# Feature blocks inside the sort rounds, half the count sums from PSUM, and two head rows loaded earlier

## What is computed

```python
x = layernorm(x + gat(x))          # 8 heads of 64: softmax over in-edges, batch norm, gelu, skip product
x = layernorm(x + tensor_prod(x))  # per-edge MLP (8 -> 64 -> 64 -> 64 -> 512), products with x[src], sum by dst
x = layernorm(x + kan_gat(x))      # one-head attention, then silu and 8 spline bases, each times 512 x 512
x = layernorm(x + sage(x))         # mean of neighbours, product 512 x 1024, relu
```

## Time and profile before

| what | before |
| --- | --- |
| median of 3 runs | 1746.64 us (1743.93 to 1747.52) |
| profiled execution: time | 1744.53 us |
| profiled execution: span | 1742.6 us |
| busy: TensorE, VectorE, ScalarE, GpSimd | 1470.6, 1321.9, 727.0, 499.8 us |
| mean granted clock of TensorE | 0.932 of full |

### The profile page before, as it was taken

How to read it: one execution, slowest core, us unless ns; L and a number is a source line. 1 busy time by engine, 2 the same in 40 slices (tenths; PEclk the granted TensorE clock), 3 DMA queues, 4 the chain that set the end, 5 groups by cost and what they waited for, 6 DMA issues and landing times.

```text
span 1742.6 us, 24098 instructions
## 1 busy us (share of the span) xinstructions
PE 1470.6 (84%) x7759; PEld 794.3 (46%) x7759; DVE 1321.9 (76%) x2036; ACT 727.0 (42%) x1595; POOL 499.8 (29%) x490
## 2 busy tenths in 40 slices
PE   2888998174878783799999999869899989999997
PEld 1465545022433332655655555745444434444443
DVE  8796999968999998499998999788377357724232
ACT  1285664075555553455554555431244134312000
POOL 1788888700010001255665664000000000002000
PEclk9889998587999996899999999979999999999999
DMA  4101000143120201455665666001011121210000
GB/s 150 31 6 9 6 6 6 35 144 87 55 73 30 72 15 39 136 169 172 189 182 166 180 190 123 1 0 49 0 58 62 48 73 48 72 72 0 12 18 29
DMA packets 67195, 122.74 MB, mean 70 GB/s; under 512 B 12613, under 2 KB 31159, under 8 KB 67010
## 3 DMA queue, kind: packets, MB, share of 16 engines
q0 software_dynamic: 22944, 58.12, 13.3%
q1 hardware_dynamic: 42748, 59.87, 10.6%
q10 hardware_dynamic: 1446, 4.03, 0.7%
HBM read 106.57 MB, written 15.22 MB: 70 GB/s over the span
## 4 chain that ended last, share of the span: by engine, by line
PE 48%; DVE 19%; POOL 14%; issue 11%; ACT 4%; DMA 3%; DVEq 1%; SPq 0%; ACTq 0%; another core or an unknown queue 0%; POOLq 0%
PE PS L1175 18%; POOL recs L641 14%; PE PS L1060 7%; DVE arena L1811 6%; PE PS L1223 5%; PE PS L1143 5%; PE PS L1046 4%; DVE arena L1807 3%; ACT arena L1486 2%; PE PS L1219 2%; PE PS L1211 2%; DVE arena L1775 2%; DVE arena L1947 1%; PE PS L1111 1%; DVE cnt_d L1581 1%
## 5 line engine op out<-in xcount | busy, mean ns | idle before, releaser
L1175 PE MATMUL PS<-arena 128*125 128x512 f32 x720 | 314.4, 600 | 12.1 <-ACT arena L1545 6.6
L641 POOL DMA_INDIRECT recs<-arena x170 | 249.0, 1464 | 90.6 <-issue 90.0
L1486 ACT ACTIVATE arena<-arena,gslot 128x32 f32<-128x32 f32 x832 | 185.3, 308 | 170.9 <-DVE arena L1930 81.6
L1060 PE MATMUL PS<-arena 128*32 128x128 f32 (+1 forms) x3328 | 231.3, 308 | 18.4 <-issue 7.9
L688 POOL DMA_INDIRECT arena<-xup,gidx x208 | 197.6, 950 | 141.8 <-DVE arena L1939 62.0
L1060 PEld LDWEIGHTS PS<-arena 128*32 128x32 f32 x3328 | 174.5, 110 | 127.5 <-issue 73.3
L977 PE MATMUL PS<-arena 125*128 125x512 f32 (+1 forms) x480 | 190.6, 535 | 44.0 <-DVE arena L1811 44.0
L1175 PEld LDWEIGHTS PS<-arena 128*125 128x125 f32 x720 | 136.8, 190 | 189.2 <-issue 189.2
L1939 DVE TENSOR_TENSOR arena<-PS,arena 128x768 f32<-128x768 f32 x208 | 196.7, 946 | 0.0
L695 POOL CAST arena<-cnt_s 125x1250 f32<-125x1250 uint16 x10 | 12.6, 1303 | 495.3 <-PE PS L1175 495.3
L977 PEld LDWEIGHTS PS<-arena 125*128 125x128 f32 x480 | 86.1, 192 | 148.5 <-issue 78.2
(11 more groups left out here) (311 smaller groups left out, 2008.2 us busy)
## 6 DMA issues: line engine op xcount, KB each, us to landing
arena<-in_spline_wT SPq DMA_DIRECT2D x16, 1024.0 KB, 5.3
arena<-uv_rows SPq DMA_DIRECT2D x14, 610.4 KB
arena<-h_rows SPq DMA_DIRECT2D x26, 256.0 KB
h_rows<-arena SPq DMA_DIRECT2D x24, 256.0 KB, 2.8
arena<-xup,gidx POOLq DMA_INDIRECT x208
recs<-arena POOLq DMA_INDIRECT x170
xup<-arena SPq DMA_DIRECT2D x10, 250.0 KB
out<-x_sb SPq DMA_DIRECT2D x10, 250.0 KB
```

What stands on the lines that cost most here:

```text
L641: pool.indirect_dma_start(out=recs, out_offset=bass.IndirectOffsetOnAxis(pos[:, c:c + 1], 0), in_=rec[:, c, :], in_offset=None).then_inc(s ...
L1060: ins = t.matmul(PS[quad * DB:(quad + 1) * DB, bank, o0 * MUL:o0 * MUL + w], sel4[:, s, v * DB:(v + 1) * DB], prod[:, s, c0 * MUL:c1 * MUL ...
L1175: ins = t.matmul(PS[:NP, b, :], basis[:, slot, (k * HB + b) * NP:(k * HB + b + 1) * NP], w_sp[:, slot, k * D:(k + 1) * D], start=(first an ...
L1486: ins = A(sel4[:, s, y * DB:(y + 1) * DB], eq4[:, m // 4, s * DB:(s + 1) * DB], ACT.Copy, scale=gslot[:, par, c + R_Y + y:c + R_Y + y + 1])
```

## The change

The sort's feature blocks 6 to 9 move into the rounds, after rounds 1, 4, 7 and 10 (`GIN`), with their copies one round later on ScalarE. In the last TAIL = 4 rounds VectorE writes `lane_dl` itself, with a float16 copy of `dl1`. Of the count sums, the even pairs still go through ScalarE and `cnt_ev` (two buffers now); the odd ones VectorE adds to `cnt_d` straight from PSUM. The rows of heads 6 and 7 are loaded after pieces 1 and 5 of the MLP, not 9 and 15. The first loads of `gld` and `h3` stand ahead of the `xup` writes in SyncE's queue. GpSimd zeroes `acc` when the last product of the attention is done, not after the first gelu half.

```diff
@@
 SBUFS = 3
+TAIL = 4
+GIN = (1, 4, 7, 10)
 NSPL = 8
@@
         PR = SB // 2
-        dl1 = at(6200, [NP, EC])
+        dl1, dl1_h = at(6200, [NP, EC]), at(6374, [NP, EC], f16)
         iota2 = sb("iota2", [128, 2 * NT], f16)
@@
         rec_sb = at(9300, [128, NDG, 2 * GT * RW])
-        cnt_ev = at(28300, [NP, 3, HALF], u16)
+        cnt_ev = at(28300, [NP, 2, HALF], u16)
+
+        def bucket_sums(n):
+            return PS[:NP, 2 * (n % 3):2 * (n % 3) + 2, :].rearrange("p a n -> p (a n)")[:, 0:HALF]
@@
                 hidden_out(n)
-                if n in (9, 15):
-                    load_row(HROWS + 2 + (n - 9) // 6)
+                if n in (1, 5):
+                    load_row(HROWS + 2 + n // 5)
             sp.wait_ge(s_uvrow_ok, 1)
@@
             sp.dma_start(a2r[:], a["L2_gnn_a"].rearrange("(r p) k -> r (p k)", p=128)).then_inc(s_wl2_in, 16)
-            for b in range(NB):
-                sp.wait_ge(s_xup_cp, b + 1)
-                sp.dma_start(xup[b * NP:(b + 1) * NP, :], xup_st[:, b % 2, :]).then_inc(s_xup_out0 if b % 2 == 0 else s_xup_out1, 16)
-
             def load_h3(pair, par):
@@
                 load_h3(par, par)
+            for b in range(NB):
+                sp.wait_ge(s_xup_cp, b + 1)
+                sp.dma_start(xup[b * NP:(b + 1) * NP, :], xup_st[:, b % 2, :]).then_inc(s_xup_out0 if b % 2 == 0 else s_xup_out1, 16)
             with sp.Fori(0, G // 4 - 1) as i:
@@
-            pool.wait_ge(s_gelu_ok, 1)
+            pool.wait_ge(s_pv_done, WR + H * NB)
             pool.memset(acc, 0.0).then_inc(s_acc_zero, 1)
@@
                 pe.wait_ge(s_sort_ok, j + 1)
-                pe.wait_ge(s_lane_cp, j + 1)
+                pe.wait_ge(s_lane_cp, min(j + 1, ROUNDS - TAIL))
                 for n in range(SB):
@@
             gat_block(HB)
-            for b in range(HB + 1, NB - 2):
-                gat_block(b)
             pe.wait_ge(s_order_cp, 2)
                 sort_batch(j)
-                if j in (3, 8):
-                    gat_block(NB - 2 + j // 8)
+                if j in GIN:
+                    gat_block(NB - len(GIN) + GIN.index(j))
                 if j == ROUNDS - 4:
@@
                     pe.wait_ge(s_oha_ok, n // WP + 1)
-                if n >= 3:
-                    pe.wait_ge(s_cnt_left, n - 2)
+                if n >= 3 and (n - 3) % 2 == 0:
+                    pe.wait_ge(s_cnt_left, (n - 3) // 2 + 1)
+                elif n >= 3:
+                    pe.wait_ge(s_cnt_flushed, n - 2)
                 for e in range(2):
@@
                 ins.then_inc(s_cntt_ps, 1)
-            pe.wait_ge(s_cnt_left, NPAIR)
+            pe.wait_ge(s_cnt_flushed, NPAIR)
             max_rows(0)
@@
-            for b in range(HB, NB - 2):
-                gat_out(b)
+            gat_out(HB)
@@
             for j in range(ROUNDS):
-                scale_lanes(j)
-                if j in (4, 9):
-                    gat_out(NB - 2 + j // 9)
+                if j < ROUNDS - TAIL:
+                    scale_lanes(j)
+                if j - 1 in GIN:
+                    gat_out(NB - len(GIN) + GIN.index(j - 1))
                 if j == ROUNDS - 3:
@@
                 act.wait_ge(s_cnt_ps, n + 1)
-                if n >= 3:
-                    act.wait_ge(s_cnt_flushed, n - 2)
-                psv = PS[:NP, 2 * (n % 3):2 * (n % 3) + 2, :].rearrange("p a n -> p (a n)")[:, 0:HALF]
-                A(cnt_ev[:, n % 3, :], psv, ACT.Copy).then_inc(s_cnt_left, 1)
+                if n >= 4:
+                    act.wait_ge(s_cnt_flushed, n - 3)
+                A(cnt_ev[:, n // 2 % 2, :], bucket_sums(n), ACT.Copy).then_inc(s_cnt_left, 1)
             for n in range(NPAIR):
-                counts_out(n)
+                if n % 2 == 0:
+                    counts_out(n)
                 if n == 1:
@@
             v.tensor_copy(tile_f, tile_i)
+            v.tensor_copy(dl1_h, dl1)
             link(v.tensor_copy(lane_f, lane_i))
@@
                 dve.wait_ge(s_lane_ok, j + 1)
+                if j >= ROUNDS - TAIL:
+                    v.tensor_tensor(lane_dl[:, rs], lane_oh[:, rs], of_pairs(dl1_h, 128), ALU.mult)
                 v.tensor_tensor(lane_src[:, rs], lane_oh[:, rs], of_pairs(src_f, 128), ALU.mult).then_inc(s_sort_ok, 1)
@@
             def flush_counts(n, word):
-                dve.wait_ge(s_cnt_left, n + 1)
+                if n % 2 == 0:
+                    dve.wait_ge(s_cnt_left, n // 2 + 1)
+                else:
+                    dve.wait_ge(s_cnt_ps, n + 1)
                 if n >= 1:
                 dstv = cnt_d[:, bass.ds(k * HALF, HALF)]
-                v.tensor_tensor(dstv, cnt_ev[:, n % 3, :], dstv, ALU.add).then_inc(s_cnt_flushed, 1)
+                v.tensor_tensor(dstv, cnt_ev[:, n // 2 % 2, :] if n % 2 == 0 else bucket_sums(n), dstv, ALU.add)\
+                    .then_inc(s_cnt_flushed, 1)
             for n in range(NPAIR + 2):
                     dst_onehots(n // WP)
```

## The result

The kernel after takes 1749.38 us in the median of 19 runs, the kernel before 1744.48 in the 19 runs beside it. The ratio is 1.0027, with a 95% interval of 1.0014 to 1.0040: 4.7 us slower (2.4 to 7.0). The forecast was 1742.5 us and, for likeliest, faster. In changes, 4.1 us less was forecast and 4.7 more came. The time lies inside the range of 1731 to 1752, the sign is wrong. The profiled execution took 1746.28 us (span 1744.4), 1.8 more than that of before.

The account below looks back on a forecast made before the run. Before the attention, VectorE's line (rounds, counts, maxima) raced scatter, load and MLP, VectorE 12 us behind. Terms: attention +0.5, zeroing -3.4, queue -1.2, sum -4.1 us; 1746.64 - 4.1 = 1742.5, range 1731 to 1752.

Parts of the forecast that it names:

- Counts: Count stage on VectorE: 52 odd sums read from PSUM take 799 instead of 476 ns, 16.8 us more.
- The bound of 22: Upper bound in us on the extra cost of the counts, if each PSUM sum also waits 0.1 for TensorE.
- The prediction's own sign of being wrong: Count stage: a PSUM sum well under 800 ns, or a subtraction that waits for the memset, would show the forecast wrong.
- Sort: Sort rounds: TensorE ends at 140.4 instead of 142.5, taken as -2.3 us on VectorE's line, bounds 0 and -6.8.
- Rows of heads 6 and 7: Maxima and MLP: 14.24 us of standing go, but MLP writes queue behind row 7; attention +0.5 us.
- Zeroing: Before layer 1's first scaling: the memset, moved to 662.6, leaves the chain, -3.4 us, no cost beside subtractions and inversion.
- a memset that blocks the subtractions or the inversion: Rival at the moved memset: subtractions wait, sum +7.1 us (1753.7), or only the inversion, +5.0 (1751.6); chance 0.15.
- Queue before the messages: Start of the message loop: with `gld` loaded long before, copies and first gather come earlier, -1.2 us, bounds 0 and -1.4.
- Cheap PSUM sums: Rival in the counts: extra below 2 us, sum -16.9, time 1729.7; with half the extra, 1734; chance 0.19.
- The stand in SyncE's queue costs more: Rival before the attention: PSUM sums cost 22 us or write backlog delays ScalarE; sum -1 to +1.5, 1745.6 to 1748; chance 0.16.
- The base: Starting time for the whole kernel: the profiled execution, 1744.53 us, with the median of the runs 2.1 above, 1746.64.

## Why the prediction failed, point by point

**Counts: the term that was mis-sized, and the cause of the wrong sign.** The sum had 16.8 us, priced from the earlier trace rows as 0.323 x 52. That price was right: (794 - 476) ns x 52 = 16.5 us. The step that failed is the next one: it took this for the whole growth of the stage and held everything else in it constant, with no term for the instructions beside the sums. There was the error: the one-hots beside it went from 389 to 425 ns, 0.036 x 208 = 7.5 us, and 16.5 + 7.5 = 24.0 is what the stage grew in the profiled pair, with other differences below 1 us.

One pair is not the typical one. The kernel before took 127.9 us for the stage in its own profile and 129.0 to 130.2 in the six others with all sums by ScalarE and the full scatter, and the five profiled runs with sums from PSUM beside the full scatter took 150.1 to 151.9, so the typical growth is nearer 21. It is made of the 16.5, of 6.5 for the one-hots (420 to 425 ns against 388 to 394), less some 2 us of shorter waits before the sums (4.8 to 5.8 us against 7.0 to 8.1, and 6.1 in the profile of before). The bound of 22 nearly allowed for it, but as a wait for TensorE in each sum, which did not occur: the idle time before the PSUM sums is 3.9 us in all, 3.5 of it one wait at the start. The experiment with all sums by ScalarE shows the price in the time itself, 22 us. The prediction's own sign of being wrong, a PSUM sum well under 800 ns, looked at the sum alone, and did not appear.

**Sort.** -2.3 was said for VectorE's line, -1.1 was seen at the start of the counts (143.39 against 144.46), less than that start differs between the six profiled executions of the old sort (142.70 to 145.87). ScalarE's part came as worked out, its last scaling ends at 125.6 (126.0 said); the rest up to TensorE's last product took 15.7 us instead of 14.5. By itself the edit gives -3.5 (-0.9 to -6.1) in the time. In the profiles 1.4 to 1.9 us of it are seen at the start of the attention, by way of an earlier MLP, which the working did not have.

**Rows of heads 6 and 7.** Right in both halves. The 14.24 us of standing went, and the price in SyncE's queue came as described: row 7 behind head 5, the writes behind row 7, ScalarE in front of a silu. The working had the attention 38.2 us behind the end of head 5 (389.2 to 427.4; its own 419.6 and 8.0 us add up to 427.6). Counted as there, to the end of the copy (395.49 + 0.17 = 395.66), 37.1 are measured. It said 15 us of standing on ScalarE and 5.86 came, because the MLP had started 15 us later, with head 3. That tie was overlooked, and the run with head 3 from memory shows that it cost nothing. So the miss at this place, 432.74 instead of 427.4, is the lateness of head 5, 395.66 instead of 389.2, less the 1.1 by which the rest was shorter. The 6.5 us of lateness are 7.2 in the counts and 1.2 in the sort, less 1.9 between the last sum and head 5. These 1.9 are no effect of the change that could be told: the stretch takes 100.3 to 103.0 us in the twelve profiles of the table.

**Zeroing.** -3.4 was said; -3.7 in the stretch by itself, 5.6 (2.8 to 8.2) in the time. The rival, a memset that blocks the subtractions or the inversion, is out: 2.06 and 7.97 us with and without it. Its price was worked out wrongly: if the subtractions wait 7.8 us, the first scaling is still free of the memset, so the 3.4 should have stayed in its sum, which gives +3.7 and not +7.1, and +1.6 and not +5.0 for the inversion. And the reason given for the inversion, that it has one input, can't be the reason: the scaling of the earlier trace rows has one tensor input in SBUF as well and took 3.93 us beside the memset. Why the one is held up and the other not, no run here shows. The Trainium skill (SBUF — State Buffer, Who interferes with whom) has it that an instruction with two SBUF inputs contends only with GpSimd instructions that read SBUF; by that rule a memset leaves the subtractions alone, and the trace agrees with 2.06 us.

**Queue before the messages.** -1.2 was said, -0.8 measured by itself, and both late edits together give -4.4 instead of -4.6.

**The base.** A second error, of some 3.7 us, lies in taking one execution for the kernel. In the profiled execution of before, the attention started at 426.84; in the two kernels whose program up to there is the same (zeroing alone, queue alone) it started at 422.87 and 423.38, with head 6 at 385.60 and 385.99 instead of 388.93. Against these two the changed kernel is 9.6 us late at the attention and, less 4.4, 5.2 late behind it, which fits the 4.7 of the runs better than the 1.8 of the two spans.

**The rivals.** Cheap PSUM sums: out, 794 ns. The memset: out. "The stand in SyncE's queue costs more", at a PSUM price of 22 us, came nearest with 1745.6 to 1748. Even so the measured 4.7 us more lie outside its -1 to +1.5. It had the line right, both ends hanging on head 5, and nearly the size of the stage's growth, 22 against a typical 21; a dearer sum as the reason was wrong, it is the one-hots beside the sums.

## What to carry to other kernels

Moving a copy from one engine to the busiest one is to be priced twice: the longer instruction, and what the neighbours of the freed or changed access lose. Where an engine stands for a transfer, first take away the stand and measure, before other work is spent on the slack; here the earlier rows alone were worth 9.8 us and the sums from PSUM cost 22. And a loss in one place is to be followed to the one event on which both lines hang (here the end of head 5), because on the other line a start that moved by 13 us changed nothing.

## What the runs showed of the hardware

While half of the sums read PSUM, the scatter's transfers get shorter and the one-hots longer. GpSimd's and VectorE's timelines around 200 us, in the changed kernel:

```profile
201.29 1.26 POOL L645 DMA_INDIRECT recs<-arena  x1 [0.30 <-issue]
202.85 1.18 POOL L645 DMA_INDIRECT recs<-arena  x1 [0.30 <-issue]
204.34 1.18 POOL L645 DMA_INDIRECT recs<-arena  x1 [0.30 <-issue]
```

```profile
201.42 0.79 DVE L1740 TENSOR_TENSOR cnt_d<-PS,cnt_d 125x626 f32 x1
202.14 0.82 DVE L1727 TENSOR_SCALAR arena<-iota_src,srt_s 128x626 bf16<-128x626 f16 x2
202.88 0.49 DVE L1740 TENSOR_TENSOR cnt_d<-arena,cnt_d 125x626 uint16 x1
203.29 0.86 DVE L1727 TENSOR_SCALAR arena<-iota_src,srt_s 128x626 bf16<-128x626 f16 x2
```

and in the kernel before:

```profile
200.83 1.66 POOL L641 DMA_INDIRECT recs<-arena  x1 [0.31 <-issue]
202.80 1.65 POOL L641 DMA_INDIRECT recs<-arena  x1 [0.30 <-issue]
```

```profile
202.34 0.67 DVE L1720 TENSOR_SCALAR arena<-iota_src,srt_s 128x626 bf16<-128x626 f16 x2
202.92 0.47 DVE L1730 TENSOR_TENSOR cnt_d<-arena,cnt_d 125x626 uint16 x1
```

A transfer's issue takes mostly 1.26 or 1.66 us before and mostly 1.18 to 1.27 after; at the same time pairs of one-hots take 0.82 and 0.86 instead of 0.67. Over the stretch from 150 to 260 us a transfer takes 1.38 to 1.43 us where all sums have both inputs in SBUF and 1.25 to 1.27 where half of them come from PSUM, and the last one is issued at 332.8 to 336.0 instead of 340.4 to 345.9. Only half of this is shown: that the one-hots lose their extra time when the transfers are gone. That the transfers gain because the sums read less from SBUF is an inference from the two groups of kernels; no run isolates it. Nor does any run show why the one-hots, which differ in nothing themselves, pay for it. The faster scatter was worth nothing here, since TensorE entered the MLP with head 3.

Two chips can differ. The one of the last runs ran the kernel before 1.7% faster, with the same start: in the changed kernel with row 7 after piece 7 the first gather leaves at 726.56, as at 726.69 in the changed kernel on a slower chip, and the 30 us lie behind it (span 1714.1 against 1744.4, granted clock 0.945 and 0.944). Most of them lie in the message loop of layer 1: from the first gather to the last it is 320.0 us against 348.4. What makes it shorter was not followed.
